# Two staging buffers in place of one between the routing matmuls and the quarter copies of a graph network kernel

## What is computed

```python
h = relu(layernorm(x))
msg = relu(concat(h[dst], edge_attr) @ W1a + b1a) @ W1b + b1b     # one row per edge
agg = segment_sum(msg, src) / max(count(src), 1)                  # src is random
out = x + relu(concat(h, agg) @ W2a + b2a) @ W2b + b2b
```

## Time and profile before

| | us |
|---|---|
| median of 3 executions | 1493.0 |
| lowest and highest | 1477.75 and 1494.9 |
| the profiled execution | 1496.89 |
| its span from first to last instruction | 1495.1 |
| mean granted TensorE clock in it | 0.943 of full speed |

### The profile page before, as it was taken

One profiled execution on the slowest core, in us unless ns is written; L12 is line 12 of the kernel. 1 busy time (PEld: TensorE's weight loads), 2 busy tenths in 40 slices (PEclk: granted clock), 3 DMA queues, 4 the chain that ended last, 5 costly groups with the idle time before them and its releaser, 6 DMA issues. The chain is left out here.

```text
span 1495.1 us, 64007 instructions
## 1 busy us (share of the span) xinstructions
PE 1254.7 (84%) x26084; PEld 1188.2 (79%) x26084; DVE 1298.6 (87%) x4459; ACT 644.6 (43%) x1429; POOL 1057.6 (71%) x702
## 2 busy tenths in 40 slices
PE   3555889889889889888889889899988989888867
PEld 3455789888888889888878779888878889888765
DVE  7886799897889889897989789899989999798787
ACT  6234444444445344444444444444534444344305
POOL 3978786775758686676868586686868668586724
PEclk9778999999999999998999999999999999899999
DMA  5769788886879798796978687787978878787552
GB/s 158 273 163 193 159 181 166 168 171 145 166 152 185 164 183 169 158 189 133 187 161 175 152 173 170 157 178 171 188 151 185 169 161 193 139 189 142 104 160 81
DMA packets 243297, 249.02 MB, mean 167 GB/s; under 512 B 151959, under 2 KB 192664, under 8 KB 241848
## 3 DMA queue, kind: packets, MB, share of 16 engines
q1 hardware_dynamic: 154744, 217.80, 53.5%
q0 software_dynamic: 88256, 27.10, 23.0%
HBM read 140.75 MB, written 31.76 MB: 115 GB/s over the span
## 5 line engine op out<-in xcount | busy, mean ns | idle before, releaser
L733 POOL DMA_INDIRECT sums<-vv,sidx x606 | 969.7, 1600 | 373.2 <-DVE sidx L1222 180.7
L1693 PE MATMUL rank_ps<-area,loop 128*128 128x65 bf16 x17640 | 660.6, 196 | 7.8 <-DVE loop L1248 4.7
L1693 PEld LDWEIGHTS rank_ps<-area,loop 128*128 128x128 bf16 x17640 | 636.6, 100 | 11.1 <-DVE loop L1248 5.8
L1678 PE MATMUL rank_ps<-r_d,oh 128*128 128x196 bf16 x2880 | 387.0, 262 | 165.1 <-ACT loop L973 155.7
L973 ACT ACTIVATE loop<-rank_ps 128x392 bf16<-128x392 f32 x720 | 346.4, 497 | 265.3 <-DMA area<-loop 183.3
L1248 DVE TENSOR_SCALAR loop<-iota,local 128x512 bf16<-128x512 int16 (+1 forms) x1440 | 438.5, 372 | 4.2
L1678 PEld LDWEIGHTS rank_ps<-r_d,oh 128*128 128x128 bf16 x2880 | 237.9, 101 | 209.6 <-ACT loop L973 181.9
L1231 DVE TENSOR_SCALAR oh<-iota,rank 128x384 bf16<-128x384 int16 x960 | 255.9, 337 | 15.0 <-PE rank_ps L1678 15.0
L951 ACT ACTIVATE r_d<-z_ps 128x512 f32<-128x512 f32 x258 | 154.5, 599 | 142.2 <-PE z_ps L1648 118.5
L962 ACT ACTIVATE vv<-c_ps 128x396 f32<-128x396 f32 x101 | 50.6, 501 | 282.0 <-PE c_ps L1667 276.2
L1256 DVE TENSOR_TENSOR dense<-rank_ps,dense 128x260 f32<-128x260 f32 x240 | 102.1, 426 | 74.7 <-PE rank_ps L1693 74.1
(11 more groups left out here) (208 smaller groups left out, 848.5 us busy)
## 6 DMA issues: line engine op xcount, KB each, us to landing
area<-loop SPq DMA_DIRECT2D x420, 147.0 KB
ids_s<-ids SPq DMA_DIRECT2D x202, 192.0 KB
et_d<-in_e_t SPq DMA_DIRECT2D x120, 256.0 KB
ids_d<-ids SPq DMA_DIRECT2D x120, 256.0 KB
et_s<-in_e_t SPq DMA_DIRECT2D x101, 192.0 KB
sums<-vv,sidx POOLq DMA_INDIRECT x606
sums<-dense POOLq DMA_DIRECT2D x4, 1625.0 KB
area<-loop SPq DMA_DIRECT2D x40, 110.2 KB
```

The source lines that it names most:

```text
L733: nc.gpsimd.indirect_dma_start(out=sums[t][:, :], out_offset=bass.IndirectOffsetOnAxis(ap=index, axis=0), in_=rows, in_offset=None, comput ...
L1678: ins = nc.tensor.matmul(l1_ps[f % 2][:, i * RW:(i + 1) * RW], oh1[:, k, block * P:(block + 1) * P], halves(DN, t)[:, k, :], start=k == si ...
L1693: ins = nc.tensor.matmul(l2_ps[h][:, u * W:u * W + w], oh2[h][:, g % MACRO, u * P:(u + 1) * P], rows[:, PARTS[r]:PARTS[r] + w], start=g % ...
```

## The change

A second staging buffer of the same size is allocated. Even groups use the old region, odd groups the new one, and each of the two has its own counter. The first eviction of a group waits for the sets that left the same buffer, the last of which is that of two groups before; groups 0 and 1 wait for none. L1239 waits for both counters, and so does SyncE before it reads `x` back into `loop`. The copies keep their number, their sizes and their place in SyncE's queue. To stay within the number of counters, `digit_step` is merged into `lane_step`. In the changed file the same lines lie 2 to 6 further down.

```diff
-SKEWED_UP_TO = tuple(16 * sum(len(skews(k)) for k in range(g)) for g in range(DENSE + 1))
+def landed_copies(g, slot):
+
+    return 16 * sum(len(skews(k)) for k in range(slot, g, 2))
...
-        staged = loop_words(0, n_staged).bitcast(bf16).rearrange("p (x c) -> p x c", c=RW)
+        staged = [a.bitcast(bf16).rearrange("p (x c) -> p x c", c=RW) for a in (loop_words(0, n_staged), sb("staged", [P, n_staged])[:])]
...
-        lane_step, bias_ready, place_step, digit_step = sems("lane_step bias_ready place_step digit_step")
+        lane_step, bias_ready, place_step = sems("lane_step bias_ready place_step")
...
-        skewed, x_back = sems("skewed x_back")
+        skewed = [sem(f"skewed{slot}") for slot in range(2)]
+        x_back = sem("x_back")
...
-                                     staged[lanes, first * BLOCKS:last * BLOCKS, :].rearrange("p x c -> p (x c)")).then_inc(skewed, 16)
+                                     staged[t.mod(2)][lanes, first * BLOCKS:last * BLOCKS, :].rearrange("p x c -> p (x c)")).then_inc(skewed[t.mod(2)], 16)
...
-                sp.wait_ge(skewed, SKEWED_UP_TO[DENSE])
+                for slot in range(2):
+                    sp.wait_ge(skewed[slot], landed_copies(DENSE, slot))
...
-                            if f == 0 and t.base:
-                                act.wait_ge(skewed, SKEWED_UP_TO[t.base])
-                            nc.scalar.activation(staged[:, 2 * f:2 * f + 2, :], bank, ACT.Copy).then_inc(routed_ready, 1)
+                            if f == 0 and t.base > 1:
+                                act.wait_ge(skewed[t.mod(2)], landed_copies(t.base, t.mod(2)))
+                            nc.scalar.activation(staged[t.mod(2)][:, 2 * f:2 * f + 2, :], bank, ACT.Copy).then_inc(routed_ready, 1)
...
-                    dve.wait_ge(skewed, SKEWED_UP_TO[(macro.base + 1) * MACRO])
+                    for slot in range(2):
+                        dve.wait_ge(skewed[slot], landed_copies((macro.base + 1) * MACRO, slot))
...
-                    dve.wait_ge(digit_step, 4)
+                    dve.wait_ge(lane_step, 13)
```

More of the change, by code:

```diff
@@ L702, in _ @@
                 pool.wait_ge(lane_step, 9)
[L703 to L707, removed]
+                nc.gpsimd.tensor_scalar(digits[:, :, :, 0], by_tile(bucket_b), -float(UNITS), None, ALU.mult).then_inc(lane_step, 1)
+                nc.gpsimd.tensor_scalar(digits[:, :, :, 1], by_tile(lane), P - 1.0, 1.0, ALU.min, ALU.add).then_inc(lane_step, 1)
+                pool.wait_ge(lane_step, 11)
+                nc.gpsimd.tensor_tensor(digits[:, :, :, 0], digits[:, :, :, 0], by_tile(column), ALU.add).then_inc(lane_step, 1)
+                nc.gpsimd.tensor_tensor(digits[:, :, :, 1], digits[:, :, :, 1], by_tile(over), ALU.add).then_inc(lane_step, 1)
                 pool.wait_ge(low_ready, done(NTURNS))
@@ L1496, in general @@
                     dve.wait_ge(place_step, PLACED)
-                    dve.wait_ge(digit_step, 4)
+                    dve.wait_ge(lane_step, 13)
                     step(nc.vector.memset(oh1[:], 0.0))
                     step(nc.vector.memset(words(0, n_routed), 0.0))
-                    step(nc.vector.memset(loop_words(0, n_staged), 0.0))
+                    for slot in range(2):
+                        step(nc.vector.memset(staged[slot], 0.0))
                     step(nc.vector.memset(loop_words(first_oh2, n_oh2), 0.0))
```

## The result

The changed kernel takes 1416.8 us (median of 4 executions, 1413.32 to 1417.63) where the kernel before takes 1488.2 (4 executions, 1477.75 to 1494.9): a ratio of 0.952, 95% interval 0.946 to 0.959. Twice more the two kernels ran side by side on one chip, with ratios of 0.943 (0.932 to 0.954) and 0.954 (0.947 to 0.960). Some executions of a kernel take longer at a lower granted clock; the ratios leave these out. The forecast was 1410 us, with 1398 to 1426 for the likeliest case. The profiled executions, 1496.89 and 1417.63 us, lie 79.3 us apart; 83 were forecast.

A forecast was written before the change was run, and what follows sets the result against it. VectorE has the highest floor, so its idle time is what can be won: 68 (steady stretch) + 10 (first groups) + 5 (end) = 83 us off 1493.0, giving 1410 us; likeliest case 1398 to 1426, wider range 1385 to 1450.

The forecast's parts named there:

- The eviction's waits all go: ScalarE's first eviction of a routed group (L973) stops waiting for copies; all 183.3 us of waits go.
- VectorE becomes the bound: In the steady rounds VectorE has the highest floor, 59.8 us a round, against 56.4 for TensorE and 56.8 for GpSimd.
- The steady stretch, 68 us: 221 to 1350 us, 17 rounds of six groups: VectorE's idle time falls from 6.6 to 2.6 us a round, winning 68.
- The first groups, 10 us: 93 to 221 us: savings before 140 us mostly given back to GpSimd's scatters; two later stalls win 10 us.
- The end, 5 us: 1350 to 1450 us: one more steady-like round gives 4 us, the last six groups 1 more.
- TensorE's clock: TensorE's granted clock rises from 0.96 to about 0.99; little hangs on it.
- Rival A: Where rounds open, the copy wait stays at 3.1 us; 56 us won in all, 1437 us; chance 0.14.
- B: Where rounds open, the waits for copies and sums both shrink to about 0.7 us; 1385 us; chance 0.10.
- C: SyncE's queue or the rows ScalarE may keep ahead of GpSimd hold each group to 11 us; about 1480 us; chance 0.08.
- D: GpSimd becomes the bound, its scatters slowed to 2.0 us by a busier VectorE; 1527 us; chance 0.04.
- the change shortens nothing of that chain but the stall ahead of it: At openings, closing copies' issue and landing before L1239 stay; the stall shrinks 1.2 us a group, leaving 1.9 of 3.1.

The follow-up runs named there:

- the second queue alone: Changed kernel with three of the seven closing copies issued on ScalarE's queue, SyncE's order left alone: 1411.5 us against 1418.7 for the changed kernel.

## Why the prediction was right

The time, the sign and the main steps held: 79.3 us were won in the profiled executions where 83 were summed up. By parts of the sum:

- **The eviction's waits all go.** Shown: none is left after the change, and all of the gain goes when they are put back.
- **VectorE becomes the bound.** Shown by the added work: 55 to 67 of 82 us appear after the change, against 12 to 20 of 56 us for TensorE.
- **The steady stretch, 68 us.** From the first fill of group 12 to that of group 114 it was 1129.7 us and is 1059.3: 70.4 won. VectorE's busy time a round stayed at 59.0, its waits fell from 6.6 to 2.6, which is the number forecast. The whole of it is in openings, as was forecast, but for 0.1 behind them. For the copies at openings 1.9 was worked out and 35.2/17 = 2.1 measured; with the sums, 2.2 was forecast in an opening and 0.4 behind it, and it was 2.5 and 0.1. So the exact 2.6 is luck in part. So is the 2.2: it was taken from the opening at 1156.36 "since its copies were the least delayed", and they weren't. They started 0.9 us behind the last eviction (1149.91 behind 1149.02), where in eight of the 17 closing groups they started 0.03 behind it; The wait there was short because VectorE itself came late to L1239. That holds for the changed kernel in general. Its copies landed about 0.7 us later behind the last eviction than before, yet VectorE came 1.8 us later (table above), and so the wait shrank by about 1.1.
- **The first groups, 10 us.** 6.1 were won (group 12 begins at 214.6 us in place of 220.7). The step was right, GpSimd's scatters hold ScalarE, and it shows as a wait that wasn't there before:

```profile
135.24 0.50 ACT L966 ACTIVATE vv<-c_ps 128x396 f32<-128x396 f32 x1 [7.86 <-POOLq L785]
...
146.94 0.49 DVE L1185 TENSOR_SCALAR hots_d<-ids_d,basew 128x1024 bf16<-128x1024 int16 x1 [4.48 <-DMA ids_d<-ids]
...
151.18 0.18 DVE L1244 SCALAR_TENSOR_TENSOR local<-area 128x12 f32<-128x12 bf16 x1 [3.75 <-DMA area<-staged]
```

  What was mis-sized is what comes behind 140 us. The 15.0 us of waits for routed groups (L1231) did go, but 6.6 us of waits for ids came, the second row being the longest, and 3.5 us for the rows that ScalarE kept late. The ids came from a queue that had fallen behind: the copies that follow them start at 144.94, and the last eviction of their group had ended at 140.61. The third row isn't new; the kernel before has 3.9 us at the same place.
- **The end, 5 us.** 2.7 won.
- **TensorE's clock.** 0.98 in the steady stretch where about 0.99 was forecast. The ten drops that are left in the stretch, 3.4 us each, all lie in opening groups, where VectorE waits for copies and TensorE for its tiles.
- **Rival A** falls: the copy wait a round went from 3.1 to 2.1 and not on at 3.1. **B** falls too: 2.6 us a round are left, not 1.1. **C** falls, with 10.4 us a group in place of 11, though SyncE's queue, which it named, does cost something (below). **D** falls: GpSimd's busy time in the stretch is 817.90 us for as many scatters as before (819.20), though VectorE is busy for 95% of it, 1003.10 of 1059. The Trainium skill, "SBUF — State Buffer", section "SBUF: two separate sides", has GpSimd locked out and unable to write the descriptors of its DMAs while VectorE runs an operation that takes the shared port pair; by that rule a denser VectorE would stretch the scatters. This isn't seen here: the shortest and the median scatter took 1546 and 1572 ns before and 1547 and 1577 after. What the traces show is the other direction. In the stretch after the change 86 of the 816 slot instructions (L1235) end 1.1 to 1.3 us after a scatter starts, and they take about 614 ns each where the median is 309. Over all of VectorE's one-hot instructions such long ones add up to about 77 us of its 1003 (an estimate: what is above each form's median), and about 78 before. So the scatters seem to cost something on the engine that bounds, as much before the change as after it; that they cause it is read from the times alone, and no run takes them away.

One step was too short, though the sum didn't suffer: "the change shortens nothing of that chain but the stall ahead of it" took SyncE's queue as free. It is nearly full. In the steady stretch it waited for other engines for 173.1 of 1129 us before and for 88.4 of 1059 after, so it works for about 9.5 us of a group's 10.4. With shorter groups it falls behind in the middle of a round: the copies start 0.0 us behind the last eviction in opening groups, 0.7 in the next and 1.2 to 1.6 in the other four, where before the change no position had a mean above 0.6. In the 17 closing groups from 17 to 113 it is 1.3 us on the average and 3.0 at the worst, where it had been 0.3 and 1.5. Ids and copies first, with the second queue, gave 24 us; the second queue alone gave 7, of which its trace shows nothing, and the new order on top of it 17. The order without the second queue wasn't run, so what it gives by itself is open.

## What to carry to other kernels

When two engines hand work through one buffer, and a transfer stands between, compare the idle time of the fullest engine with the stall: it is the fullest engine's idle time that a second buffer returns (here 79 us for 183 us of stalls), and work added to that engine tells beforehand how much is idle at least (here 77 us). After such a change read the issuing queue's own order: a wait on a DMA may be a wait for the queue to reach it. What is needed first should be issued first, in pieces if need be, here ids before copies before the rest.

## What was not expected

Before the change, VectorE at 87% busy took 77 us more work, 6% of its own, for no time at all. A share of busy time said nothing of what it bounds.

Part of the wait for the closing copies was SyncE standing at other issues, whose busy time no row of the page counts. Taking three of the seven copies off its queue ended the issue 1.4 us earlier and brought the last landing no earlier; letting them start 1.2 us earlier as well brought L1239 forward by 1.4 us and gave 17 us more. What is left to win there is small: L1239 now starts 0.5 us after VectorE is ready for it.
